# Sums of a first norm that arrive already spread over the partitions, with logarithm and exponential in place in PSUM, in a transformer layer with routed experts

## The reference

```python
x0 = up_part(relu(down_part(x))) + x                       # adapter, per sequence
h  = attn_norm_w * x0 * rsqrt(mean(x0 * x0, -1) + 1e-5)    # the first norm
q, k, v = split(h @ qkv_w + qkv_b)                         # 16 heads, 4 key and value heads of 64
attn = exp(logits - logaddexp(logsumexp(logits), sink))    # causal, rotary positions
x1 = x0 + attn @ v @ proj_w + proj_b
h2 = rmsnorm(x1)                                           # the second norm
out = x + x1 + sum over the 4 best experts of gate * (silu(h2 @ Wg) * (h2 @ Wu) @ Wd)
```

## Time and profile before

| | |
|---|---|
| Time, median of 3 runs | 1138.51 us (1137.43 to 1142.05) |
| Time of the profiled execution | 1133.5 us |
| Its span, first to last instruction | 1131.7 us |
| TensorE busy | 984.0 us (87%) |
| VectorE busy | 829.8 us (73%) |
| GpSimd busy | 700.9 us (62%) |
| ScalarE busy | 456.6 us (40%) |
| Mean granted clock of TensorE | 0.918 of full |

### The profile page before, as it was taken

The page is one execution under the profiler, slowest core; times in us unless marked ns, Lnnn a source line. Parts: engine busy times, 40 slices in busy tenths (PEclk is TensorE's granted clock), DMA queues, the critical chain, the costliest instruction groups (busy, mean ns, idle before and its releaser), DMA issues.

```text
span 1131.7 us, 19754 instructions
## 1 busy us (share of the span) xinstructions
PE 984.0 (87%) x6270; PEld 795.6 (70%) x6270; DVE 829.8 (73%) x1750; ACT 456.6 (40%) x1120; POOL 700.9 (62%) x654
## 2 busy tenths in 40 slices
PE   3879699998999989989987419999999999999995
PEld 2557477676776776757766308888888888888884
DVE  3878589778787788877957526777777677777778
ACT  1123243342432423333344205555555555555541
POOL 1404435757747667576585856777777777777750
PEclk8779799889898898988999659999999999999997
DMA  6237976566566555574665467776776767766599
GB/s 188 69 87 237 326 255 187 157 198 179 176 181 207 161 167 190 179 217 136 186 204 194 154 231 261 266 257 246 255 245 212 250 228 250 257 212 209 133 336 372
DMA packets 110748, 239.22 MB, mean 211 GB/s; under 512 B 19170, under 2 KB 48247, under 8 KB 109914
## 3 DMA queue, kind: packets, MB, share of 16 engines
q1 hardware_dynamic: 84042, 192.03, 51.8%
q0 software_dynamic: 19552, 40.02, 11.1%
q10 hardware_dynamic: 7056, 5.91, 1.6%
HBM read 140.37 MB, written 90.05 MB: 204 GB/s over the span
## 4 chain that ended last, share of the span: by engine, by line
PE 38%; DVE 22%; POOL 18%; issue 14%; DMA 6%; ACT 1%; SPq 0%; DVEq 0%; POOLq 0%; ACTq 0%
POOL rows_in L685 7%; PE gbank L985 7%; PE gbank L852 6%; DVE ring L1354 6%; POOL pick_rows L692 4%; POOL lists L647 4%; PE scores L813 4%; DMA rows_in<-x_rows,token_row 4%; PE gbank L1005 3%; PE gbank L777 3%; PE gbank L748 2%; POOL ring L654 1%; DVE stat L1368 1%; PE gbank L767 1%; DVE prob L1390 1%
## 5 line engine op out<-in xcount | busy, mean ns | idle before, releaser
L985 PE MATMUL gbank<-ring,in_part 128*128 x954 | 262.8, 411 | 0.1
L654 POOL TENSOR_TENSOR ring<-ring 128x512 fp32r<-128x512 f32 x96 | 121.5, 1281 | 141.7 <-ACT ring L1151 141.1
L692 POOL DMA_INDIRECT pick_rows<-rows_out,pair_row x156 | 161.6, 1036 | 56.5 <-issue 46.9
L985 PEld LDWEIGHTS gbank<-ring,in_part 128*128 128x128 f32 x954 | 168.6, 190 | 28.7 <-issue 0.3
L685 POOL DMA_INDIRECT rows_in<-x_rows,token_row x156 | 151.7, 972 | 54.2 <-issue 34.3
L647 POOL DMA_INDIRECT lists<-entry,slot_i x128 | 136.1, 1063 | 36.7 <-issue 34.1
L1005 PE MATMUL gbank<-ring,mid_part 128*128 x954 | 151.3, 294 | 0.4 <-DVE mid_part L1609 0.4
L1588 DVE SCALAR_TENSOR_TENSOR in_part<-scores,norm_w,in_part 128x128 fp32r<-128x128 f32 x318 | 96.8, 346 | 53.2 <-ACT in_part L1196 53.1
L1597 DVE SCALAR_TENSOR_TENSOR mid<-gbank,norms,silu 128x256 f32<-128x256 f32 x156 | 75.5, 484 | 74.4 <-ACT silu L1204 73.0
L852 PE MATMUL gbank<-w_o,ring 128*128 128x256 f32 x512 | 126.3, 403 | 0.6 <-ACT ring L1121 0.6
L777 PE MATMUL gbank<-h_t,w_qk 128*128 128x512 f32 x480 | 122.1, 405 | 4.7 <-DVE ring L1354 2.5
(11 more groups left out here) (171 smaller groups left out, 1553.1 us busy)
## 6 DMA issues: line engine op xcount, KB each, us to landing
w_parts<-ring SPq DMA_DIRECT2D x192, 256.0 KB, 3.2
ring<-w_parts SPq DMA_DIRECT2D x32, 1536.0 KB
ring<-in_W_up SPq DMA_DIRECT2D x64, 256.0 KB, 4.1
q_r<-rot SPq DMA_DIRECT2D x32, 512.0 KB, 6.1
picks<-pick_rows SPq DMA_DIRECT2D x8, 2048.0 KB, 22.2
lists<-in_fill_slots SPq DMA_DIRECT2D x36, 256.0 KB, 5.2
ring<-in_W_down SPq DMA_DIRECT2D x32, 256.0 KB, 3.9
x_t<-in_x_t SPq DMA_DIRECT2D x8, 512.0 KB, 4.9
```

Of the source, the lines that this page charges most:

```text
L654: e.tensor_tensor(lower, lower.bitcast(F32), upper.bitcast(F32), ALU.subtract).then_inc(s_lower, 1)
L692: e.indirect_dma_start(out=pick_rows, out_offset=bass.IndirectOffsetOnAxis(ap=begun_row[:, i:i + 1] if i < AHEAD else pair_row[:, i:i + 1] ...
L985: ins = e.matmul(bank[:, :], in_parts[i % 2][x][:, c, :], ring[:, bass.ds(at + y * WE + c * 2 * DFF, 2 * DFF)], start=k == 0, stop=k == le ...
```

## The change

`sums` on TensorE becomes two products of a 128x128 square of ones with the squares, 128x512 each, added up in one bank; the first waits only for the first half of the squares. The sum of each token then stands on all 128 partitions at once. Logarithm and exponential work on that bank in place, on 128x512 values. VectorE's `apply` reads the bank. The identity products (L1331), the product of `apply` (L767), the buffer `rms1` and two semaphores go. `apply` leaves TensorE's lists, and with it one bank in the round; `sums` leaves VectorE's. All lists are new.

```diff
 ORDERS = {
     "PE": ("""
-        down cond up sums apply pair pair pair pair pair down value score up
+        down cond up sums pair pair pair pair pair down value score up
     """, """
-        value score turn_prob score sums attend apply route_turn project pair route_turn turn_prob pair
-        score route_turn route_turn attend route_pick value pair route_count project pair turn_prob
-        attend pair value value project turn_prob down attend score up project
+        value turn_prob score sums attend score route_turn project pair route_turn turn_prob pair score
+        route_turn route_turn attend route_pick value pair route_count project pair turn_prob attend
+        pair value project value turn_prob down attend score up project
...
     "DVE": ("""
...
-        softmax_a value sums softmax_b apply project pair softmax_a pair softmax_b route_pick value pair
+        softmax_a value apply softmax_b project pair softmax_a pair softmax_b route_pick value pair
...
...
     "ACT": ("""
...
-        attend softmax_a split turn_prob split project split down attend split softmax_a up split
+        attend split softmax_a turn_prob split project split down attend split softmax_a up split
...
-        turn_prob softmax_a root attend split route_turn split split split project route_turn turn_prob
+        softmax_a root split turn_prob attend route_turn split split split project route_turn turn_prob
...
     "POOL": ("""
...
-        split split pair split split pair pair split split pair split pair route_put split split
-        route_put split up route_put split split route_put
+        split split pair split split pair pair split split pair split pair route_put split route_put
+        split split up route_put split route_put split
...
     "SP": ("""
-        load_x_t load_late load_third load_third load_middle load_third load_x_t move move move move
+        load_x_t load_late load_third load_middle load_third load_x_t move move load_third move move
... 
         def norm1_sums(m, banks):
-            w.wait_ge(s_sq, KC * m + KC)
             bank = take(banks[0])
-            for s in range(TPM):
-                for c in range(KC):
-                    ins = e.matmul(bank[:, s:s + 1], tmp[0][c][:, s * P:(s + 1) * P], ones[:, 0:1],
-                                   start=c == 0, stop=c == KC - 1)
+            for c in range(KC):
+                w.wait_ge(s_sq, KC * m + c + 1)
+
+                ins = e.matmul(bank[:, :], ones[:, :], tmp[0][c][:, :], start=c == 0, stop=c == KC - 1)
             ins.then_inc(s_ssq1, 1)
-            freed[banks[0]] = (s_log1, m + 1)
-
-        def norm1_apply(m, banks):
-            w.wait_ge(s_diag, m + 1)
-            bank = take(banks[0])
-            e.matmul(bank[:, :], ones[:, :], tmp[0][2][:, :], start=True, stop=True).then_inc(s_spread, 1)
             freed[banks[0]] = (s_normed, KC * m + KC)
...
-            e.activation(rms1[:, 0, :], gbank[banks[0]][:, 0:TPM], ACT.Ln, bias=eps[:, 0:1], scale=1.0 / D).then_inc(s_log1, 1)
+            e.activation(bank[:, :], bank[:, :], ACT.Ln, bias=eps[:, 0:1], scale=1.0 / D).then_inc(s_log1, 1)
             w.wait_ge(s_log1, m + 1)
-            e.activation(rms1[:, 1, :], rms1[:, 0, :], ACT.Exp, scale=-0.5).then_inc(s_rms1, 1)
+            e.activation(bank[:, :], bank[:, :], ACT.Exp, scale=-0.5).then_inc(s_rms1, 1)
...
-        def norm1_sums(m):
+        def norm1_apply(m, banks):
             w.wait_ge(s_rms1, m + 1)
-            w.wait_ge(s_middle, MIDDLE)
-            w.wait_ge(s_act, m + 1)
-            for s in range(TPM):
-                ins = e.tensor_scalar(tmp[0][2][:, s * P:(s + 1) * P], ident[:, :], rms1[:, 1, s:s + 1], None, ALU.mult)
-            ins.then_inc(s_diag, 1)
-
-        def norm1_apply(m, banks):
-            w.wait_ge(s_spread, m + 1)
             for c in range(KC):
                 e.tensor_tensor(tmp[0][c][:, :], x0_t[m % 2][:, c, :], gbank[banks[0]][:, :], ALU.mult).then_inc(s_normed, 1)
```

More of the change, by code:

```diff
@@ L78 @@
     "DVE": ("""
-        cond down up weights sums apply pair pair pair pair pair constants down value softmax_a
-        softmax_b up
+        cond down up weights apply pair pair pair pair pair constants down value softmax_a softmax_b up
     """, """
-        softmax_a value sums softmax_b apply project pair softmax_a pair softmax_b route_pick value pair
+        softmax_a value apply softmax_b project pair softmax_a pair softmax_b route_pick value pair
         route_count project route_list pair softmax_a pair value softmax_b project value down softmax_a
@@ L105 @@
     """, """
-        split split pair split split pair pair split split pair split pair route_put split split
-        route_put split up route_put split split route_put
+        split split pair split split pair pair split split pair split pair route_put split route_put
+        split split up route_put split route_put split
     """, """
-        split split split split split split route_put split route_put split route_put split split
-        route_put split route_put split route_put route_put route_put
+        split split split split split route_put split split route_put split route_put split split split
+        route_put split route_put route_put route_put route_put
     """),
     "SP": ("""
-        load_x_t load_late load_third load_third load_middle load_third load_x_t move move move move
+        load_x_t load_late load_third load_middle load_third load_x_t move move load_third move move
         move
     """, """
-        load_x_t fill_lists fill_lists fill_lists store_third fill_lists load_third store_third
-        fill_lists move fill_lists store_third fill_lists load_third fill_lists load_third fill_lists
+        fill_lists fill_lists fill_lists load_x_t fill_lists store_third fill_lists load_third
+        store_third fill_lists fill_lists move store_third fill_lists load_third load_third fill_lists
         fill_lists fill_lists fill_lists move fill_lists fill_lists load_third fill_lists store_x2
-        fill_lists fill_lists store_third load_third move fill_lists fill_lists store_third store_third
-        fill_lists fill_lists move fill_lists store_x2 fill_lists fill_lists load_third fill_lists move
+        fill_lists fill_lists store_third load_third move fill_lists fill_lists fill_lists store_third
+        store_third fill_lists move fill_lists move fill_lists store_x2 fill_lists load_third fill_lists
         load_third fill_lists store_third fill_lists load_third fill_lists load_third fill_lists
         store_third store_third fill_lists store_x2 fill_lists store_third fill_lists load_third
-        fill_lists store_third fill_lists load_third fill_lists store_third fill_lists load_third
-        fill_lists store_x2 fill_lists
+        fill_lists store_third fill_lists load_third fill_lists store_x2 fill_lists load_third
+        fill_lists store_third fill_lists
     """, """
@@ L136 @@
 ROOT_OF = [m if m < NM - 1 else NM - 1 + (0, 0, 1, 2)[s] for m in range(NM) for s in range(TPM)]
-BANKS_OF = {"cond": 1, "down": 1, "up": KC + 1, "sums": 1, "apply": 1, "pair": 2, "value": 1,
+BANKS_OF = {"cond": 1, "down": 1, "up": KC + 1, "sums": 1, "pair": 2, "value": 1,
             "turn_prob": 2, "attend": 2, "project": 1, "route_turn": 1, "route_pick": 1, "route_count": 1}
@@ L398, in program @@
     s_picks = [sem(f"s_picks{i}") for i in range(NPICK)]
-    (s_cond, s_down, s_up, s_ssq1, s_spread, s_qk, s_v, s_scores, s_pt, s_pv, s_proj, s_x2_turn, s_gate,
+    (s_cond, s_down, s_up, s_ssq1, s_qk, s_v, s_scores, s_pt, s_pv, s_proj, s_x2_turn, s_gate,
      s_count) = (sem(f"s_{n}") for n in (
-         "cond", "down", "up", "ssq1", "spread", "qk", "v", "scores", "pt", "pv", "proj", "x2_turn", "gate",
+         "cond", "down", "up", "ssq1", "qk", "v", "scores", "pt", "pv", "proj", "x2_turn", "gate",
          "count"))
@@ L1086, in norm1_sums @@
         def norm1_sums(m, banks):
+            bank = gbank[banks[0]]
             w.wait_ge(s_ssq1, m + 1)
             w.wait_ge(s_memset, ONES)
[L1089 to L1091 removed]
+            e.activation(bank[:, :], bank[:, :], ACT.Ln, bias=eps[:, 0:1], scale=1.0 / D).then_inc(s_log1, 1)
             w.wait_ge(s_log1, m + 1)
[L1093 removed]
+            e.activation(bank[:, :], bank[:, :], ACT.Exp, scale=-0.5).then_inc(s_rms1, 1)
         def norm1_apply(m):
@@ L1485, in vector_program @@
                 constants()
-            elif name == "sums":
-                norm1_sums(k)
             elif name == "apply":
-                norm1_apply(k, banks)
+                norm1_apply(k, banks_for["sums", k])
             elif name == "pair":
```

7 lines of the change are left out of this document (2 added, 5 removed).

## The result

The changed kernel takes 1144.10 us (median of 22 runs, 1133.99 to 1150.21), the kernel before beside it 1137.24 us (22 runs). The ratio is 1.0051, with an interval from 1.0034 to 1.0068. Forecast were 1112 us and a range of 1100 to 1130; the change gives nothing and costs half a per cent. The profiled execution took 1140.84 us, span 1139.0, against 1133.5 and 1131.7 before.

The account below looks back on a forecast made before the run. No engine is full; a chain of waits through PE and DVE, with PE nearly alone around the norm, bounds the kernel. Gains 15 + 2.9 + 3.6 + 5 = 26.5 us gave 1112 us from the median of 1138.5, range 1100 to 1130.

Parts of the forecast that it names:

- the marks that the prediction set for the norm: Periods 2 to 6: `sums` near 1.9 us, pair 7.7 behind value tile, L852 near 3.6, full clock, functions near 0.6.
- Rival (a): Clock still falls around the norm, slowing `score` and `project`: 16 us back, 1128 us; chance 0.22 with its smaller kin.
- The marks for the whole period: Period near 69.5 us; idle before the last score product near 1.1 us, and near 3 in period 0.
- The step that failed: Period 4's norm on DVE: `softmax_b` behind `apply` ends at 381.4, beside `project`; first pair begins at 381.3, 3.3 us earlier.
- such a collision: Just before the last pair's move, one DVE operation with two splits becomes one with a single split; nothing counted.
- The 15 us that the norms were to give: Norms together, 14.9 us of it from first pairs starting earlier in periods 2 to 6; bounds about 2 and 21 us.
- The start: At the kernel's start everything waits for the norm; L1337 starts at 32.16 instead of 35.10, 2.9 us gained.
- The norm of period 0: L852 already ran near full clock and the value tile came late, leaving no gain: -0.2 us.
- The last pair's move, periods 1 to 6: The move and the score product needing it come 0.6 us earlier per period: 3.6 us, bounds 0 and 10.
- In period 0 the term: Last pair's move in period 0 issues at once on SP: 5 us gained, between 3.6 and 8.24.
- Rival (d): Load behind the move lands late, ACT stands at its split, `down`'s act and `up` follow: 1145 us; chance 0.06.
- the 26.5: Total forecast gain in us: norms 15, start 2.9, last pair's move 3.6 in periods 1 to 6 and 5 in period 0.

Follow-up runs that it names:

- softmax_first: The changed kernel with `softmax_b` ahead of `apply` again on VectorE in the period: 1137.50 us, ratio 0.9993 to the kernel before.
- one_swap: The changed kernel with the last two steps of GpSimd's period swapped (`route_put split` became `split route_put`): 1127.21 us, ratio 0.9904 to the kernel before.
- pool_before: The changed kernel with GpSimd's lists of before: 1124.67 us, ratio 0.9904 to the kernel before.
- load_first: The changed kernel with GpSimd's lists of before and SP's new list in period 0 only: 1117.34 us, ratio 0.9824 to the kernel before.
- before_new_pool: The kernel before with only GpSimd's lists replaced by those of the changed kernel: 1148.13 us, ratio 1.0098 to the kernel before.
- norm_only: The new norm with the lists of before, without `apply` on PE and `sums` on DVE: 1135.74 us, ratio 1.0005 to the kernel before.

## Why the prediction was wrong

**The norm, right in its own terms.** Pair 7.74 us behind the value tile, `sums` 1.98, L843 3.62, clock at full, functions 0.64 and 0.58: the marks that the prediction set for the norm hold. Summed from 84 to 580 us, the granted clock is at half for 51 us, where it was 83. Rival (a) is out. The marks for the whole period do not hold: from the first rotation of chunk 5 to that of chunk 6 it is 74.9 us, where it was 72.3 and 69.5 was forecast, and the idle time before period 4's last score product is 1.95 us (1.1 forecast).

**The step that failed** is in the same part: "`softmax_b`, now behind `apply`, ends at 381.4 and lies beside `project`". That took L1366 at its 0.2 us. It stands 2.8 to 4.1 us behind three splits, and what it delays is the rotation of the pair, on the path. I had seen such a collision ("of one DVE operation with two splits on POOL") and costed it where it stood, at nothing, but not asked where GpSimd's new list would put the row of splits. Its last step and the first two of the next period make three in a row, and the new norm brings the addition just there. The table shows where the time went over chunks 2 to 7, in us against the kernel before (plus is longer). The squares are counted from the start of their first instruction. Each row is one execution, which can lie a few us off the median.

| | `up` to squares | squares to first pair | first pair to its rotation | together |
|---|---|---|---|---|
| after | +6.8 | -12.8 | +12.0 | +6.1 |
| softmax_first | +9.9 | +1.1 | 0.0 | +11.0 |
| one_swap | +6.9 | -16.9 | 0.0 | -10.0 |
| pool_before | +6.4 | -16.9 | 0.0 | -10.6 |
| load_first | +1.3 | -15.7 | 0.0 | -14.4 |

The 15 us that the norms were to give are there between the squares and the first pair, nearly so in the kernel after and in full with GpSimd's lists of before. The prediction put the two stretches on either side at nothing. The one behind the pair costs 12.0 us and goes with one swap on GpSimd. The one ahead of the squares costs 6 to 7 us, most of which goes with SP's list of before.

**The start,** 2.9 forecast, 3.3 measured.

**The norm of period 0,** costed at -0.2 us, lost 3.1. TensorE was at half clock there, and the two products of `sums` then take 3.78 us together (78.02 to 81.80), where L759 took 1.95. The sum had used 1.88, a full-clock row, for a place at half clock. The `score` ahead of it took 3.68 us for 2.00 as well.

**The last pair's move, periods 1 to 6,** 3.6 us forecast, nothing measured. From the pair's last result on GpSimd to the score product it was 7.21 to 7.47 us in periods 1 to 5 before, and is 7.68 to 8.59 after. The idle time in front of the product adds up to 10.3 us in those five periods, for 9.2. Transfers follow the move at once in both kernels (a load and a store before, a store and two loads after); what makes it slower was not tried. In period 0 the term was right (6.1 for 5).

**Rival (d)** had the right sign and time (1145) by a mechanism that is there but small: ScalarE waits 4.66 us for the load, which puts the act 0.51 us behind the score product. pool_before keeps SP's lists and ScalarE's wait (5.01 us in period 3) and is faster by 17 us, so it is not the cause. It does cost something: load_first, without that wait, is 9 us faster still by the ratios, and 5 us of that lie between `up` and the squares in the table. The wait also brings splits together, as the 3.03 us of L1351 in the kernel after show, where GpSimd's list lets them.

**The sum as the runs have it,** by the ratios: the new norm alone 0; with the new lists of all engines but GpSimd, -11 us; GpSimd's new list on top, +17; that list in the old kernel, +11. The change had a gain, and one engine's list took it and a little more. What was forecast beyond these 11 us is the 4.4 that the stretches of chunks 2 to 7 fall short (10.6 for 15), the 3.1 of period 0's norm, and the 3.6 of the move; some 4 us of the 26.5 stay without a name.

The best version is `load_first`, the new norm with GpSimd's lists of before and SP's early move in period 0 alone: 1117.34 us, 1.8% less than before.

## What to carry to other kernels

When two engines' orders are changed together, lay the new rows of long GpSimd instructions beside VectorE's instructions with inputs in SBUF, the small ones too, and look at what is queued behind these; a wait that was free where it stood isn't free where the new order puts it. Look across the edge from one period to the next: the last and the first steps make a row that neither line of the list shows. And take a product's duration from a row at the clock of the place where it will stand.

## What the runs showed of the hardware

A VectorE instruction on 128x16 values, both inputs in SBUF, took 2.80 to 4.10 us in place of 0.18 beside a row of two-input GpSimd instructions of 1.26 us each. It ended with the last of the row (386.22 and 386.19; 234.53 and 234.48), not with the first. The maximum with zero (L1351), which has one such input, does the same beside two splits (361.43 and 361.39), and in before_new_pool a 128x512 instruction (L1341) took 4.5 us for 0.69 beside three. L1363 (1.21 us), L1357 (1.22) and L1334 (0.68 each) kept their durations where splits ran beside them; of these, L1363 has one input and the other two read PSUM as well. L1370, whose two inputs both lie in SBUF, met one split in the kernel after and took 3.01 us for 1.22. The Trainium skill (SBUF — State Buffer, Who interferes with whom) says that a VectorE instruction with two SBUF inputs contends with a GpSimd instruction that reads SBUF, and, of VectorE's two-port modes, that whoever issues first has the shared ports for the whole instruction. The trace agrees that the two exclude each other; the wait is for up to three instructions, which the section does not say. Being first did not help VectorE here. By the recorded starts L1370 had begun 0.65 us ahead of its split (590.64 and 591.29), and 0.42 us ahead in pool_before, and the addition of period 2 began 0.28 us ahead of the row (230.43 and 230.71); the splits kept their length, and the VectorE instruction ended last. Between halves of 256 columns the addition was let in after 0.43 us. Why there and not between whole splits stays open.

Cutting a GpSimd instruction of 512 columns in two costs 0.17 to 0.24 us per pair of halves (1.44 to 1.51 us for 1.27).

The clock stayed at full after the wide `sums` across a wait of 1.38 us. It fell within a wait of 3.27 us in norm_only, and in softmax_first after waits of 1.37 and 1.11 us that ended at 378.57 and 383.61 (0.54 in the window at 384 us). So a fall does not need the one-column products, and the length of one wait alone does not decide it.
